# A graph network's edge counts: source one-hots over four quarters and windows of 32 targets instead of halves and windows of 64

## The reference

```
h = relu(layernorm(x))
q, k, v = h@Wq + bq, h@Wk + bk, h@Wv + bv
adj[src, dst] = 1
x1 = x + softmax(where(adj, q@k.T / sqrt(512), -1e6)) @ v
h = relu(layernorm(x1))
deg[dst] = 1 + number of edges with that dst        # the 1 is a self loop
agg(z)[s] = sum over edges s->d of z[d] / sqrt(deg[s]*deg[d])
out = x1 + agg(relu(batchnorm(agg(h@W1 + b1))) @ W2 + b2)
```

## Time and profile before

| | |
|---|---|
| median of 3 runs | 347.08 us (346.77 to 347.77) |
| the profiled execution, its own time | 346.12 us |
| its span in the trace | 344.2 us |
| TensorE busy | 323.1 us, 94% of the span |
| VectorE busy | 204.3 us, 59% |
| ScalarE busy | 121.9 us, 35% |

### The profile page before, as it was taken

The page is one execution under the profiler, slowest core; times in us unless marked ns, Lnnn a source line. Parts: engine busy times, 40 slices in busy tenths (PEclk is TensorE's granted clock), DMA queues, the critical chain, the costliest instruction groups (busy, mean ns, idle before and its releaser), DMA issues.

```text
span 344.2 us, 4979 instructions
## 1 busy us (share of the span) xinstructions
PE 323.1 (94%) x1530; PEld 250.4 (73%) x1530; DVE 204.3 (59%) x463; ACT 121.9 (35%) x192; POOL 54.9 (16%) x96
## 2 busy tenths in 40 slices
PE   1489989999989999989999999999999999999996
PEld 0466655776756778768888888888778888787884
DVE  6689799998859822353644636374732238649221
ACT  2905422544574550432224333222630205425000
POOL 5113000000000045503025160202001004400000
PEclk9999999999999999999999999999999999999999
DMA  6912200000321000031001010000000000000042
GB/s 235 291 39 61 63 0 1 1 2 0 125 79 44 0 0 2 1 122 33 16 14 30 2 49 14 0 0 2 1 0 0 2 0 3 0 0 2 12 155 79
DMA packets 9030, 12.75 MB, mean 37 GB/s; under 512 B 2736, under 2 KB 2992, under 8 KB 9008
## 3 DMA queue, kind: packets, MB, share of 16 engines
q1 hardware_dynamic: 9008, 12.46, 11.0%
HBM read 10.36 MB, written 2.10 MB: 36 GB/s over the span
## 4 chain that ended last, share of the span: by engine, by line
PE 80%; DVE 8%; ACT 6%; issue 2%; POOL 2%; DVEq 1%; DMA 1%; SPq 0%; POOLq 0%; ACTq 0%
PE ps L780 18%; PE ps L781 17%; PE ps L782 17%; PE ps L853 9%; PE ps L1045 8%; PE ps L964 5%; PE ps L907 2%; DVE wA L561 1%; ACT cnt L453 1%; PE ps L928 1%; DMA xt<-x_in 1%; PE ps L801 1%; DVE bnst L749 1%; DVE g L746 1%; DVE src_oh L601 1%
## 5 line engine op out<-in xcount | busy, mean ns | idle before, releaser
L601 DVE TENSOR_SCALAR src_oh<-iota,ecol 128x512 f16 x172 | 48.9, 349 | 3.8 <-PE ps L853 2.4
L853 PE MATMUL ps<-src_oh,dst_oh 128*128 x172 | 41.1, 381 | 1.2 <-DVE dst_oh L603 1.2
L780 PE MATMUL ps<-hT,wA 128*128 128x512 f32 x64 | 26.8, 418 | 6.4 <-DVE wA L561 6.4
L853 PEld LDWEIGHTS ps<-src_oh,dst_oh 128*128 x172 | 18.3, 114 | 16.8 <-issue 4.4
L964 PE MATMUL ps<-cnt,qh 128*128 128x512 f32 x128 | 30.1, 391 | 0.1
L1045 PE MATMUL ps<-qh,cnt 128*128 128x512 f32 x128 | 29.3, 390 | 0.0
L375 ACT ACTIVATE cnt<-ps 64x512 int16<-64x512 f32 x32 | 18.9, 591 | 29.3 <-PE ps L858 28.8
L964 PEld LDWEIGHTS ps<-cnt,qh 128*128 128x128 f32 x128 | 23.9, 188 | 5.5 <-issue 0.6
L1045 PEld LDWEIGHTS ps<-qh,cnt 128*128 128x128 f32 x128 | 23.9, 188 | 5.3 <-DVE vb L761 0.3
L780 PE MATMUL ps<-v,pT 128*128 128x512 f32 x64 | 25.0, 391 | 1.0 <-DVE pT L663 1.0
L781 PE MATMUL ps<-hT,wA 128*128 128x512 f32 x64 | 25.7, 401 | 0.0
(11 more groups left out here) (151 smaller groups left out, 615.1 us busy)
## 6 DMA issues: line engine op xcount, KB each, us to landing
xt<-x_in SPq DMA_DIRECT2D x16, 256.0 KB, 2.9
out<-xt SPq DMA_DIRECT2D x8, 256.0 KB, 2.4
wA_raw<-L_gnn_Wk_in SPq DMA_DIRECT2D x2, 512.0 KB, 6.8
wB_raw<-L_gnn_Wv_in SPq DMA_DIRECT2D x2, 512.0 KB, 8.3
wA_raw<-L_gnn_Wq_in SPq DMA_DIRECT2D x2, 512.0 KB, 4.9
wB_raw<-L_gnn_W_in SPq DMA_DIRECT2D x2, 512.0 KB, 3.8
w_raw<-L_gnn_W_in SPq DMA_DIRECT2D x2, 512.0 KB, 3.7
bias_row<-L_gnn_b_in SPq DMA_DIRECT2D x2, 256.0 KB, 3.8
```

Of the source, the lines that this page charges most:

```text
L601: dve.tensor_scalar(src_oh[:, bass.ds(slot, 1), j, :].rearrange("p a n -> p (a n)"), iota[:, :], ecol[:, bass.ds(c + j, 1)], None, ALU.is_ ...
L780: pe.matmul(out_, stat(1), mov(0), start=first, stop=False)
L853: m = pe.matmul(ps[:, i % 2, :], dst_oh[:, bass.ds(slot, 1), :, j].rearrange("p a n -> p (a n)"), src_oh[:, bass.ds(slot, 1), j, :].rearra ...
```

## The change

A window is now 32 targets, and the sources go in four quarters of 256 (LOW), so that the 128 columns of a target one-hot are 4 quarters x 32 targets and a product has 256 moving columns. There are 32 windows, and two of them (one from each of two neighbouring blocks of 128 targets) share a PSUM bank as its left and right half: that is a turn, of which there are 16 as before. The source one-hots of a round are made by one `tensor_tensor` of 256 x 4, in the manner of the target one-hots. ScalarE copies a bank in four instructions of 32 x 2 x 256, and the degrees are summed by eight ScalarE instructions of their own (`degree`), which write a scratch copy to T. Two blocks become complete with every fourth turn. From the same inputs the 32 windows need 6, 3, seven times 2, 1, 2, 1, 2 and then nineteen times 1 rounds, 48 in all, so 192 products. The 16 turns have 2, 2, 2, 2, 8, 5, 4, 4, 4, 2, 3, 2, 2, 2, 2, 2 rounds.

```diff
-WIN = 64
-ORDER = (14, 15) + tuple(range(14))
+WIN = 32
+LOW = 256
+NQ = N // LOW
+TURNS = NW // 2
+TURN_PAIRS = (3, 0, 1, 2)
...
+    adj_after = lambda i: 2 * ((i - 6) // 4) + i % 4 - 2
+    def window_of(i):
+        turn, half = divmod(i, 2)
+        pair, quad = divmod(turn, 4)
+        return 4 * (2 * TURN_PAIRS[pair] + half) + quad
...
 ScalarE
-            for a in range(2):
-                act.activation(cnt16[rows, w // 2, a * HALF:(a + 1) * HALF], ps[a * WIN:(a + 1) * WIN, i % 2, :], ACT.Copy,
-                               accum_out=degp[rows, a, w // 2:w // 2 + 1]).then_inc(S["c16"], 1)
+            for a in range(NQ):
+                act.activation(cnt16[quad * WIN:(quad + 1) * WIN, t:t + 2, a * LOW:(a + 1) * LOW],
+                               ps[a * WIN:(a + 1) * WIN, turn % 2, :].rearrange("p (t n) -> p t n", t=2),
+                               ACT.Copy).then_inc(S["c16"], 1)
...
+        def degree(i):
+            b = block_of(i)
+            act.wait_ge(S["loops_added"], i + 1)
+            if i >= 2:
+                act.wait_ge(S["deg_ready"], i - 1)
+            act.activation(T[:, i % 2, :], cnt16[:, b, :], ACT.Copy,
+                           accum_out=deg[:, b:b + 1]).then_inc(S["deg_ready"], 1)
...
-            if i >= 4 and i % 2 == 0:
-                adj_out(i // 2 - 2)
+            if i >= 6 and i % 4 >= 2:
+                adj_out(adj_after(i))
+                degree(adj_after(i))
...
 VectorE, ahead of the windows
-        step(dve.tensor_scalar(edge_f[:, 1, :], edge_i[:, 1, :], float(HALF), float(N), ALU.is_ge, ALU.mult))
-        step(dve.tensor_tensor(edge_f[:, 0, :], edge_f[:, 1, :], edge_i[:, 0, :], ALU.add))
+        step(dve.tensor_scalar(edge_f[:, 1, :], edge_i[:, 1, :], float(LOW), None, ALU.is_ge))
+        for a in range(2, NQ):
+            step(dve.scalar_tensor_tensor(out=edge_f[:, 1, :], in0=edge_i[:, 1, :], scalar=float(a * LOW),
+                                          in1=edge_f[:, 1, :], op0=ALU.is_ge, op1=ALU.add))
+        step(dve.scalar_tensor_tensor(out=edge_f[:, 0, :], in0=edge_f[:, 1, :], scalar=float(N), in1=edge_i[:, 0, :],
+                                      op0=ALU.mult, op1=ALU.add))
...
 VectorE, adj_cols and a round
-            dve.wait_ge(S["c16"], 4 * (i + 1))
+            dve.wait_ge(S["c16"], 16 * (i // 2 + 1))
...
-                for j in range(UNROLL):
-                    dve.tensor_scalar(src_oh[:, bass.ds(slot, 1), j, :].rearrange("p a n -> p (a n)"), iota[:, :],
-                                      ecol[:, bass.ds(c + j, 1)], None, ALU.is_equal)
+                dve.tensor_tensor(src_oh[:, bass.ds(slot, 1), :, :].rearrange("p a n u -> p (a n) u"), iota[:, :, :],
+                                  ecol[:, bass.ds(c, UNROLL)].rearrange("p (o u) -> p o u", o=1).to_broadcast(
+                                      [P, LOW, UNROLL]), ALU.is_equal)
...
 VectorE, behind the turns
+        adj_cols(NT - 2)
         adj_cols(NT - 1)
-        step(dve.scalar_tensor_tensor(out=deg[:, :], in0=degp[:, 0, :], scalar=1.0, in1=degp[:, 1, :], op0=ALU.add,
-                                      op1=ALU.add))
+        dve.wait_ge(S["deg_ready"], NT)
...
 TensorE
-                    m = pe.matmul(ps[:, i % 2, :], dst_oh[:, bass.ds(slot, 1), :, j].rearrange("p a n -> p (a n)"),
-                                  src_oh[:, bass.ds(slot, 1), j, :].rearrange("p a n -> p (a n)"), start=False,
+                    m = pe.matmul(ps[:, turn % 2, half * LOW:(half + 1) * LOW],
+                                  dst_oh[:, bass.ds(slot, 1), :, j].rearrange("p a n -> p (a n)"),
+                                  src_oh[:, bass.ds(slot, 1), :, j].rearrange("p a n -> p (a n)"), start=False,
...
-            counts(i, now)
-            if i >= 4 and i % 2 == 0:
-                adj_turn(i // 2 - 2)
+            for half in range(2):
+                now = bounds
+                if (i, half) != (TURNS - 1, 1):
+                    bounds = bounds_of(2 * i + half + 1)
+                counts(i, half, now)
+            if i >= 6 and i % 4 >= 2:
+                adj_turn(adj_after(i))
```

More of the change, by code:

```diff
@@ L303, in _ @@
             ln1(t)
-        pool.wait_ge(S["deg_ready"], 1)
-        pw(dinv[:, :], deg[:, :], NT).then_inc(S["dinv_ready"], 1)
+        pool.wait_ge(S["deg_ready"], NT)
         def add_bv(t):
@@ L328, in _ @@
         mask_fill(1)
+        pw(dinv[:, :], deg[:, :], NT).then_inc(S["dinv_ready"], 1)
         for t in range(XT):
@@ L405, in _ @@
         act.wait_ge(S["bk_in"], 16)
-        for i in range(NW):
+        for i in range(TURNS):
             for item in ahead[i]:
@@ L418, in _ @@
         adj_out(NT - 2)
+        degree(NT - 2)
         adj_out(NT - 1)
+        degree(NT - 1)
         hi_of(("q", 1, 0))
@@ L621, in _ @@
                     lo_of(item)
-            now = bounds
-            if i + 1 < NW:
-                targets_of(i + 1)
-                bounds = bounds_of(i + 1)
-            onehots(i, now)
+            for w in (2 * i, 2 * i + 1):
+                now = bounds
+                if w + 1 < NW:
+                    targets_of(w + 1)
+                    bounds = bounds_of(w + 1)
+                onehots(w, now)
             if i < 2:
                 stats(KC + 2 * i)
-            if i >= 3 and i % 2 == 1:
-                adj_cols((i - 3) // 2)
+            if i >= 5 and (i - 5) % 4 < 2:
+                adj_cols(2 * ((i - 5) // 4) + (i - 5) % 4)
             if i == 11:
@@ L839, in bounds_of, with counts @@
         def bounds_of(i):
-            return pe.value_load(lohi[0:1, ORDER[i]:ORDER[i] + 1], min_val=256, max_val=257 * NCH)
-        def counts(i, bounds):
-            if i >= 2:
-                pe.wait_ge(S["c16"], 2 * (i - 1))
-            pe.matmul(ps[:, i % 2, 0:32], zerob[:, :], zerob[:, 0:32], start=True, stop=False, skip_group_check=True)
+            w = window_of(i)
+            return pe.value_load(lohi[0:1, w:w + 1], min_val=256, max_val=257 * NCH)
+        def counts(turn, half, bounds):
+            if half == 0:
+                if turn >= 2:
+                    pe.wait_ge(S["c16"], NQ * (turn - 1))
+                pe.matmul(ps[:, turn % 2, 0:32], zerob[:, :], zerob[:, 0:32], start=True, stop=False,
+                          skip_group_check=True)
             first, end = bounds & 255, bounds >> 8
@@ L857, in counts @@
                 pe.reg_add(used, used, 1)
-            pe.matmul(ps[:, i % 2, 0:32], zerob[:, :], zerob[:, 0:32], start=False, stop=True,
-                      skip_group_check=True).then_inc(S["c_done"], 1)
+            if half == 1:
+                pe.matmul(ps[:, turn % 2, 0:32], zerob[:, :], zerob[:, 0:32], start=False, stop=True,
+                          skip_group_check=True).then_inc(S["c_done"], 1)
         make(("h", 0, 0))
```

46 lines of the change are left out of this document (23 added, 23 removed).

## The result

The changed kernel takes 361.57 us (median of 4 runs, 359.48 to 362.12) against 347.12 us (346.77 to 347.77, 4 runs) beside it: ratio 1.0415, 95% interval 1.0375 to 1.0454. It is 14.5 us slower; 3.7 us were forecast, with 355 as the upper end. The direction was right, the size was not. The profiled execution took 361.47 us, span 359.6 against 344.2.

A forecast was written before the change was run, and what follows sets the result against it. TensorE's stream was taken as the bound, its sequencer a hidden second limit. Terms +0.5 - 1.7 + 1.0 + 1.65 - 0.7 + 3.0 = +3.75 us on 346.1 gave 349.9, the median 1.0 above: 350.8 us, range 346.5 to 355.

The forecast's parts named there:

- At half of 0.22 us each: Products of 256 columns cost half of 0.22 us, so a round drops from 0.87 to 0.44 us on the array.
- start: Ahead of the turns, two more integer steps at 0.36 us each delay the first item: +0.5 us, between 0.3 and 1.1.
- turns 0 and 1: Two items each, bound by the array, which gains from the narrower products: -1.7 us.
- turns 2 to 10: Mostly paced by TensorE's sequencer, 63.5 us in place of 62.5: +1.0 us.
- turn 11: ScalarE's chain to the split of Wq grows by four count copies and a degree instruction; TensorE waits: +1.65 us.
- turns 12 to 15: Turn 12 waits for one-hots, then three sequencer-paced turns: 19.0 us against 19.7, term -0.7 us.
- tail: Behind the last turn, transposes wait about 2.8 us for ScalarE's copies and VectorE's mask: +3.0 us, between 2.4 and 3.6.
- The 1.3 us a round: TensorE's sequencer needs 1.3 us for each round beyond the first, making turn 4's eight rounds 12.4 us.
- the third rival: Nothing to tell: late turns 4.3 us, not 4.6, sequencer's 0.4 us between turns partly a wait; 347.9 us total, chance 0.11.
- VectorE: One-hots: the 1024-element source compare costs 0.60 or 0.87 us, a round 0.94 or 1.34, hidden beside the sequencer.
- The clock: Rival: thin turns and idle tail drop the array to its lower clock, 1.8 us or more a fall; 352.6 to 358, chance 0.17.
- VectorE's pace: First rival: VectorE, not the sequencer, paces the heavy turns, turn 4 at 9.9 us; 344.3 us total, chance 0.13.

The follow-up runs named there:

- The dense kernel: Changed kernel with TensorE reading each product's moving operand as 256 neighbouring elements, not every fourth of 1024 (wrong counts): 352.21 us.
- the kernels without the dip: Changed kernel with one edit each: zero-adding products in turn 4, 363.47 us; Wq split first in turn 10, 358.02; q(1,0) ahead of the tail's transposes, 358.75.

## Why the prediction was wrong

- **Products, "At half of 0.22 us each": the step that failed.** They came at 0.228 to 0.231, because the new layout reads them at a step of 8 bytes. With dense reads the kernel takes 352.2 us, so this step alone is worth 9.4 of the 10.8 us by which the forecast missed (products and what they draw after them). The prediction took the price from the width and never asked how the columns lie; the fact was in the diff (`src_oh[..., :, j]`), and no row of before has such a moving operand. It should have been an unseen operation with bounds 0.11 and 0.22 or more.
- **The rest of the sum was right by luck in part.** The dense kernel, against the terms of the forecast: start +1.9 (+0.5), turns 0 and 1 -0.9 (-1.7), turns 2 to 10 +0.2 (+1.0), turn 11 +1.8 (+1.65), turns 12 to 15 -2.1 (-0.7), tail +5.5 (+3.0). Too cheap a start and tail and too dear a sequencer cancelled in part, and a kernel before beside it took 345.83 us, so that its loss is 6.4 us against 3.7 forecast. Two slips of arithmetic are smaller: the turns from 2 to 10 add up to 63.1 us by the prediction's own rules (8.5, 7.8 and 7.5 for turns 5, 7 and 8), a term of +0.6 and not +1.0, and its own bounds give 348.6 to 353.4.
- **The sequencer.** The 1.3 us a round held in turn 4: its round starts (L881) between 50 and 56 us in the kernel after read

```profile
L881 PEldq FUSED_REGOPS  x4: 41/41/41, 50.3 to 54.3; - x4
```

  which is 1.33 us. It was ahead of the array by then, so turn 4's eight rounds took 8.4 us there and the turn 11.8, not 12.4. The late turns took 4.73 us without transposes, close to the 4.6 for the wrong reason: the array needed them (2.84 + 1.85), and the dense read shows the sequencer at 4.2. The 0.4 us between turns was partly a wait, as the third rival had it: in the dense kernel it is 0.24, from the branch's end at 115.01 us to the load at 115.25.
- **VectorE** was right: 0.61 and 0.87 us from start to start, rounds of 0.94 and 1.34. Odd rounds cost more (0.87 against 0.61 us), against the rule of the Trainium skill that the prediction weighed (Vector Engine (DVE) Microarchitecture Reference, section 5.1).
- **The start**: +1.9 for +0.5. The two added steps took 0.65 us for both, about what was forecast; the held compare cost 1.7 to 2 us more. With the iota out of the way k's first product came at 18.16 us, as before the change (18.21). The prediction did not look at what stood beside them on GpSimd, whose iota the change made twice as large.
- **The chain of Wq**: +1.9 for +1.65. Four copies take 2.42 us, forecast 2.0; the degree 1.14.
- **The tail**: +4.7 for +3.0. The wait is 2.5 us, within the bounds; the lower clock on the transposes and q(1,0) adds 1.5 us (0.3 and 1.2), and one more set of eight transposes, which now falls behind the last turn, 0.4.
- **The clock.** It fell three times, in turns 4 to 5, at turn 12 and in the tail; the items behind took 4.46, 4.41 and 3.97 us in place of 3.25, 2.83 and 2.86 in the kernels without the dip, some 4 us in all. That rival, at a chance of 0.17, was right as a mechanism and priced a fall at 1.8 us, a little high (1.2 to 1.6 measured); at least the fall behind the tail's wait belonged into the sum, not beside it as an alternative. The prediction's counterexample (17 products in 5 us, clock 1.00) had them 512 wide.
- **VectorE's pace and nothing to tell** (the first and third rival) did not come about.

The run at 359.48 us has a mean granted clock of 0.984 where the others have 0.975. That need not be a fall fewer: the kernel with the later iota has all three falls and 0.984 too, its clock reading 1.00 over the start. What made this run shorter stays open.

## What to carry to other kernels

When a layout changes so that one wide instruction can fill an operand, price the reader too: ask for the byte step at which TensorE will read it, and give a dense and a stepped bound. A wait on TensorE can cost its length and then the lower clock on what follows: the waits of 2.4 and 2.5 us here did, at 1.2 to 1.6 us a fall, so that what looks like 2.5 us is worth 4. The wait of about 1 us ahead of turn 12 in the kernel before did not. Before moving a chain's length, look whether the order on its engine can be changed for nothing.

## What was unexpected in the hardware

- A bf16 moving operand at a step of 4 bytes runs at 0.117 us for 256 columns, dense at 0.110, at a step of 8 bytes at 0.228 to 0.231 (512 columns: 0.217 dense, 0.452 at 8 bytes).
- GpSimd's iota costs 0.34 us for a plain line of 256 numbers and, for 128x1024, 2.26 with each number repeated four times inside, 5.70 with it repeated twice inside, and holds VectorE's compare of 128x128 integers for as long as it runs (0.23 us with no iota beside it), but not the instructions that stood beside it when it came later.
- VectorE's compare of 128x1024 against a broadcast takes 0.61 us at an even first chunk in both layouts; at an odd one 0.87 with inner runs of four and 1.14 with runs of two.
